# Field attention on one core: four score tiles of a batch issued together, small products and ScalarE's copies placed anew

## What is computed

```python
qkv = (x @ Wqkv.T + bqkv).reshape(Bb, Ss, 3, H, HD).transpose(2, 0, 3, 1, 4)
q, k, v = (qkv[0], qkv[1], qkv[2])
attn = softmax(einsum('bhid,bhjd->bhij', q, k) / sqrt(HD), axis=-1)
coh = sigmoid(tanh(comb @ Wc1.T + bc1) @ Wc2.T + bc2).transpose(0, 2, 1)
mod = attn * coh[..., None]
mod = mod / (mod.sum(-1, keepdims=True) + 1e-08)
mod = (1.0 - fi) * mod + fi * fa[:, None, :, None]
out = einsum('bhij,bhjd->bhid', mod, v).transpose(0, 2, 1, 3).reshape(Bb, Ss, Ee)
return out @ Wout.T + bout
```

## Time and profile before

| | us |
|---|---|
| runs of the kernel | 1911.90, 1923.15, 5402.26 (median 1923.15) |
| span of the profiled execution | 1905.3 |
| field attention in it, first to last exponential | 743.4 to 996 |
| PE busy | 1622.1 (85%) |
| VectorE busy | 1252.2 (66%) |
| ScalarE busy | 1082.6 (57%) |
| GpSimd busy | 861.1 (45%) |

### The profile page before, as it was taken

The page is one execution under the profiler, slowest core; times in us unless marked ns, Lnnn a source line. Parts: engine busy times, 40 slices in busy tenths (PEclk is TensorE's granted clock), DMA queues, the critical chain, the costliest instruction groups (busy, mean ns, idle before and its releaser), DMA issues. The chain is left out here.

```text
span 1905.3 us, 42986 instructions
## 1 busy us (share of the span) xinstructions
PE 1622.1 (85%) x15415; PEld 1160.9 (61%) x15415; DVE 1252.2 (66%) x3295; ACT 1082.6 (57%) x3196; POOL 861.1 (45%) x1080
## 2 busy tenths in 40 slices
PE   3788629983369966999998799999999999899988
PEld 0354329982259953656567677777777777566633
DVE  7588634534454546778876877777777777467757
ACT  2444304431134423889874677777777777777653
POOL 0237746664546641434333866707162543542223
PEclk8799659995579986999989999999999999999989
DMA  2940123314122243000003422231213131221001
GB/s 69 378 150 27 37 62 114 115 56 122 36 63 73 71 129 120 24 28 24 20 21 87 102 62 65 57 73 50 74 40 77 43 87 50 71 54 43 20 13 44
DMA packets 157665, 135.73 MB, mean 71 GB/s; under 512 B 90021, under 2 KB 130278, under 8 KB 155302
## 3 DMA queue, kind: packets, MB, share of 16 engines
q1 hardware_dynamic: 146950, 113.91, 20.3%
q0 software_dynamic: 9088, 18.70, 3.0%
q10 hardware_dynamic: 1440, 0.66, 0.1%
HBM read 76.65 MB, written 56.54 MB: 70 GB/s over the span
## 5 line engine op out<-in xcount | busy, mean ns | idle before, releaser
L847 POOL DMA_INDIRECT y<-moe_y,moe_aim x156 | 177.0, 1135 | 144.5 <-DVE moe_y L987 62.8
L2874 DVE TENSOR_TENSOR delta_sv<-delta_sv,delta_zp 32x256 f32<-32x256 f32 x384 | 161.3, 420 | 111.2 <-PE delta_zp L2440 103.9
L1809 ACT ACTIVATE field_p<-field_sp,field_nm 128x128 f32<-128x128 f32 x512 | 179.9, 406 | 6.7 <-DVE field_nm L1900 6.3
L2787 POOL TENSOR_TENSOR delta_dd<-delta_dd,delta_prod 128x30 f32<-128x30 f32 (+11 forms) x270 | 165.6, 613 | 21.2
L2785 POOL TENSOR_TENSOR delta_prod<-delta_ll,delta_dd 128x30 f32<-128x30 f32 (+11 forms) x270 | 140.5, 520 | 21.2
L2780 POOL TENSOR_TENSOR delta_dd<-delta_ll,delta_minus 128x1024 f32<-128x1024 f32 (+1 forms) x9 | 22.4, 2486 | 270.6 <-DMA delta_ll<-lanes 270.5
L1809 ACT ACTIVATION_READ_ACCUMULATOR field_p<-field_sp,field_nm 128x1 f32 x512 | 126.6, 247 | 0.0
L2440 PE MATMUL delta_zp<-delta_sv,delta_ct 128*32 128x128 f32 x1536 | 121.1, 279 | 5.2 <-DVE delta_sv L2874 4.6
L2858 DVE SCALAR_TENSOR_TENSOR delta_la<-delta_xp,delta_ck,delta_dc 128x256 f32<-128x256 f32 x256 | 107.5, 476 | 3.2 <-PE delta_xp L2398 1.5
L1910 DVE COPY field_pT<-field_ptp 128x512 f32<-128x512 f32 x128 | 84.1, 672 | 33.2 <-PE field_ptp L1659 33.2
L2440 PEld LDWEIGHTS delta_zp<-delta_sv,delta_ct 128*32 128x32 f32 x1536 | 69.6, 109 | 56.2 <-issue 24.3
(11 more groups left out here) (574 smaller groups left out, 4452.3 us busy)
## 6 DMA issues: line engine op xcount, KB each, us to landing
delta_al<-alpha SPq DMA_DIRECT2D x33, 512.0 KB, 4.5
pairs<-c_none SPq DMA_DIRECT2D x16, 1032.0 KB, 17.1
moe_xg<-pairs SPq DMA_DIRECT2D x78, 129.0 KB
moe_yt<-y SPq DMA_DIRECT2D x16, 512.0 KB, 4.7
w_E<-in_E_dram SPq DMA_DIRECT2D x1, 4624.0 KB, 36.1
w_E<-in_E_dram SPq DMA_DIRECT2D x8, 578.0 KB
lanes<-delta_la SPq DMA_DIRECT2D x256, 16.0 KB, 1.5
delta_di<-inverses SPq DMA_DIRECT2D x64, 64.0 KB, 2.3
```

What stands on the lines that cost most here:

```text
L847: nc.gpsimd.indirect_dma_start(results, bass.IndirectOffsetOnAxis(ap=aim[:, t % AR, j:j + 1], axis=0), y[:, t % YS, j, :], None).then_inc( ...
L1809: last = nc.scalar.activation(p[:, slot, h, :], s_ps[i][:, k, :], ACT.Exp, bias=nm[:, slot, h:h + 1], accum_out=zs[:, slot, h:h + 1])
L2787: last = nc.gpsimd.tensor_tensor(dd[lanes, a + 1:, 0:a], dd[lanes, a + 1:, 0:a], pr, ALU.subtract)
L2874: nc.vector.tensor_tensor(sv[rows, two, :], sv[rows, two, :], z_ps[2 * pair // HH][rows, at, :], ALU.subtract).then_inc(s["z_kept"], 1)
```

## The change

PE: `scores` loses its pairs. One call issues all four tiles, and waits until all four tiles of exponentials of the batch before are done. It stands behind `turn(n, 2)` and ahead of `turn(n, 3)`. `turn_factors` goes from the end of batch 0 to its start, `project_t` from its start behind `turn(n, 1)`; the first half of coherence stays at the start of batch 1 (behind the values there); the values of batch 1 and 2 come early in their batch; both halves of `alpha_beta` move up, to either side of `turn(n, 1)` in batch 3; the values of tile 2 come ahead of the scores. ScalarE: `keep_f` moves from batch 1 to batch 0, `keep_k` one tile earlier. VectorE: all four maxima of the next batch come behind the first three copies, `norm_before` comes at the end of a batch, `keep_y` moves from batch 1 to batch 0, `keep_v` ahead of the first copy of batch 3, `norm` ahead of its last two maxima. GpSimd and SyncE are unchanged. Nothing is computed otherwise.

```diff
--- before.py
+++ after.py
@@ -1641,13 +1641,13 @@
             pe.wait_ge(s["xsum_kept"], u + 1)
             nc.tensor.matmul(xa[:, VSUM:VSUM + GB], w["WvT1"][:], xsum[:], start=True, stop=True).then_inc(s["z_made"], 1)
 
-        def scores(n, half, b, pair, group):
-            if b == 0 and pair == 0:
+        def scores(n, half, b, group):
+            if b == 0:
                 pe.wait_ge(s["q_kept"], group + 1)
-            if b < 2 and pair == 0:
+            if b < 2:
                 pe.wait_ge(s["km_made"], group * 2 + 1 + b)
-            pe.wait_ge(s["exps"], n * HQ + 2 * pair + 2 + EXPS0 - HQ)
-            for i in (2 * pair, 2 * pair + 1):
+            pe.wait_ge(s["exps"], n * HQ + EXPS0)
+            for i in range(HQ):
                 rows = slice(i * 32, (i + 1) * 32)
                 nc.tensor.matmul(s_ps[i][:], qT[rows, half, b * T:(b + 1) * T], km[rows, half, :, b * T:(b + 1) * T],
                                  start=True, stop=True).then_inc(s["s_made"], 1)
@@ -1704,8 +1704,7 @@
         project_k(0, 0)
         pe.wait_ge(s["k_kept"], 1)
         project_v(0)
-        scores(0, 0, 0, 0, 0)
-        scores(0, 0, 0, 1, 0)
+        scores(0, 0, 0, 0)
         pe.wait_ge(s["primed"], 1)
         def turn_groups(it):
             for half in range(2):
@@ -1713,56 +1712,55 @@
                 final = isinstance(it, int) and half == 1
                 for b in range(GB):
                     n = u * GB + b
-                    after = (n + 1, half, b + 1) if b < GB - 1 else (n + 1, 1 - half, 0)
                     turn(n, b % 2, 0)
-                    if not final or b < GB - 1:
-                        scores(*after, 0, u if b < GB - 1 else u + 1)
                     if b == 0:
                         pe.wait_ge(s["v_kept"], u + 1)
                         pe.wait_ge(s["h_kept"], u + H0)
+                        turn_factors(u, 1 - half)
+                        values_before(n, 1, 1 - half, GB - 1)
+                    if b == 1:
+                        pe.wait_ge(s["t_kept"], u + 1)
+                        coherence(range(GB // 2))
+                        pe.wait_ge(s["y_kept"], u + 1)
+                        pe.wait_ge(s["vm_made"], (u + 1) * GB)
+                        values_before(n, 0, half, 0)
+                    if b == 2:
+                        values_before(n, 1, half, 1)
+                    if b == 3:
+                        if not final:
+                            pe.wait_ge(s["v_kept"], u + 2)
+                        alpha_beta(u, range(GB // 2))
+                    turn(n, b % 2, 1)
+                    if b == 0:
+                        pe.wait_ge(s["f_kept"], u + 1)
                         project_t(half)
                     if b == 1:
-                        pe.wait_ge(s["t_kept"], u + 1)
-                        pe.wait_ge(s["f_kept"], u + 1)
-                        coherence(range(GB // 2))
-                    if b % 2 == 0:
-                        values_before(n, (b + 1) % 2, half if b else 1 - half, (b - 1) % GB)
+                        coherence(range(GB // 2, GB))
+                        sum_values(u)
                     if b == 2:
                         pe.wait_ge(s["z_kept"], u + 1)
                         if not final:
                             pe.wait_ge(s["k_kept"], u + 2)
                         output(u)
-                    turn(n, b % 2, 1)
-                    if b == 1:
-                        coherence(range(GB // 2, GB))
-                        sum_values(u)
-                        pe.wait_ge(s["y_kept"], u + 1)
-                        pe.wait_ge(s["vm_made"], (u + 1) * GB)
-                        values_before(n, 0, half, 0)
-                        if not final:
-                            project_q(u + 1, 1 - half, it * 16 + 16 + 16 * half, u + 1)
-                    if b == 3 and not final:
-                        pe.wait_ge(s["v_kept"], u + 2)
-                    if b == 3:
-                        alpha_beta(u, range(GB // 2))
-                    turn(n, b % 2, 2)
                     if b == 3:
                         alpha_beta(u, range(GB // 2, GB))
-                    if not final or b < GB - 1:
-                        scores(*after, 1, u if b < GB - 1 else u + 1)
+                    turn(n, b % 2, 2)
+                    if b == 1 and not final:
+                        project_q(u + 1, 1 - half, it * 16 + 16 + 16 * half, u + 1)
+                    if b == 3:
+                        values_before(n, 0, half, 2)
+                    if b < GB - 1:
+                        scores(n + 1, half, b + 1, u)
+                    elif not final:
+                        scores(n + 1, 1 - half, 0, u + 1)
                     turn(n, b % 2, 3)
-                    if b == 0:
-                        pe.wait_ge(s["t_kept"], u + 1)
-                        turn_factors(u, 1 - half)
                     if b == 1 and not final:
                         project_k(u + 1, 1 - half)
                     if b == 2 and not final:
                         pe.wait_ge(s["a_kept"], u + 1)
                         project_v(1 - half)
-                    if b == 3:
-                        values_before(n, 0, half, 2)
-                        if not final:
-                            spread_group(u)
+                    if b == 3 and not final:
+                        spread_group(u)
 
         def spread_group(u):
             pe.wait_ge(s["ba_kept"], u + 1)
@@ -1843,17 +1841,17 @@
                     n = u * GB + b
                     for i in range(HQ):
                         exp_scores(n, b % 2, i)
+                        if b == 0 and i == 1:
+                            keep_f(u)
                         if b == 0 and i == 3:
                             keep_t(u)
-                        if b == 1 and i == 1:
-                            keep_f(u)
                         if b == 1 and i == 3:
                             exp_z(u)
                             if not final:
                                 keep_q(u + 1, 1 - half)
                         if b == 2 and i == 0 and final:
                             alpha_exp(0)
-                        if b == 2 and i == 1 and not final:
+                        if b == 2 and i == 0 and not final:
                             keep_k(u + 1)
                         if b == 2 and i == 3:
                             keep_a(u)
@@ -1967,6 +1965,7 @@
         dve.sem_inc(s["pt_kept"], TURNED0)
         dve.sem_inc(s["h_kept"], H0)
         keep_v(0)
+        norm_before(0, 1)
         for i in range(HQ):
             peaks(0, 0, i)
         before = ch.n
@@ -1978,29 +1977,31 @@
                 for b in range(GB):
                     n = u * GB + b
                     now, then = b % 2, (b + 1) % 2
-                    norm_before(n, then)
                     if b == 2:
                         coherence(u, half)
-                    keep_turned(n, now, 0)
                     if b == 3 and not final:
                         dve.wait_ge(s["vm_made"], (u + 1) * GB)
                         keep_v(u + 1)
+                    keep_turned(n, now, 0)
+                    keep_turned(n, now, 1)
+                    if b == 0:
+                        keep_y(u)
+                        sum_x(u, half, it * 16 + 16)
+                    if b == 1:
+                        keep_z(u)
+                    if b == 3:
+                        keep_alpha(u)
+                    keep_turned(n, now, 2)
+                    norm_before(n + 1, now)
                     if not final or b < GB - 1:
                         for i in range(2):
                             peaks(n + 1, then, i)
-                    if b == 0:
-                        sum_x(u, half, it * 16 + 16)
-                    if b == 1:
-                        keep_y(u)
-                        keep_z(u)
-                    keep_turned(n, now, 1)
-                    keep_turned(n, now, 2)
-                    if b == 3:
-                        keep_alpha(u)
+                    keep_turned(n, now, 3)
+                    if b == 3 and not final:
+                        norm(u)
                     if not final or b < GB - 1:
                         for i in range(2, HQ):
                             peaks(n + 1, then, i)
-                    keep_turned(n, now, 3)
                     if isinstance(it, int) and half == 0:
                         diagonal(ch, range(2 * b, 2 * b + 2))
                     if final and b == 0:
@@ -2010,7 +2011,6 @@
                     if b == 3 and not final:
                         keep_c1(u + 1)
                         scale_alpha(u)
-                        norm(u)
 
         with dve.Fori(0, TURNS - 1) as it:
             ch.turn(it, 2 * LINKS, before)
@@ -2018,7 +2018,6 @@
         assert ch.n == 2 * LINKS, ch.n
         ch.turn(0, 0, before + (GROUPS - 2) * LINKS)
         turn_groups(TURNS - 1)
-        norm_before(B, 1)
         alpha_sum(0)
```

## The result

The changed kernel takes 1942.27 us (median of four runs, 1937.52 to 1946.52). The kernel before took 1911.90, 1914.14 and 1923.15 us, beside the one of 5402.26 that is no measure. Their ratio is 1.0152, with a 95% interval of 1.0123 to 1.0181: slower by 1.5%, some 29 us, and the interval leaves out 1. The forecast was 1948 us.

A forecast was written before the change was run, and what follows sets the result against it. PE's queue was taken to set the 30.58 us beat before. 8 groups x (2.2 + 2.6) = 38 us, less 8, gives +30 on 1917.5: 1948 us, range 1922 to 1973.

The forecast's parts named there:

- PE's saving: In the field stage, joining four score tiles removes 4.2 us a group from PE's queue; none need reach the end.
- The closed ring: Score tiles wait for all four exponential tiles of the batch before: 7.56 us a batch, 31.29 a group with two copies.
- PE late: PE's queue makes scores late by 0.55 us in batch 1 and 0.93 in batch 3; batches 0 and 2 on time.
- Other queues: Norm in batch 3 stays hidden: input ready about 9.2 us after the batch's first exponential, VectorE arrives at 9.5.
- Sum without drops: Field stage beat from handovers, copies and PE's lateness at full clock: 32.8 us a group, +2.2.
- Drops: PE's clock falls in nearly every batch 3, four of five batches 1, 3.4 us each: 2.6 us a group lost.
- What before pays: In the field stage the kernel before loses about 8 us to its own clock drops, subtracted from the added time.
- What would show it: ScalarE waits 1 to 2 us a batch, beat 32.8 to 36 us, PE busy below 85%, clock falling in most groups.
- the ring without drops: Rival: field stage without clock drops, 8 x 2.2 - 8 = +10 us, 1928 us; chance 0.22.
- Long drops: Rival: half or all of batch 3's clock drops last 10 us, 1962 to 1975 us; chance 0.20.
- The gain: Rival: handover costs much less, beat about 27.5 us a group, -25 us, 1893 us; chance 0.05.
- the tiles do run side by side: Rival denied this: the second score pair lands 1.06 us later, +33 us, 1950 us; chance 0.05.

The follow-up runs named there:

- e3_ahead: Changed kernel with four unread transposes a batch between the wait for the exponentials and the scores; 1.0323 of the kernel before.
- e4_behind: Changed kernel with four unread transposes a batch ahead of the first transposes, where PE waits; 1.0127 of the kernel before.
- e1_pairs: Changed kernel with scores in two pairs, the first waiting only for exponential tiles 0 and 1, and two maxima ahead of norm_before; 1.0085 of the kernel before.
- e9_values: Changed kernel with batch 3's values of tile 2 right behind the first transposes instead of ahead of the scores; 1.0102 of the kernel before.
- e2_filled: Changed kernel with unread transposes of the identity where PE would wait; 1.0051 of the kernel before.
- e5_alone: Kernel before with four score tiles together where pair 1 stood, and VectorE's first two maxima and fourth copy reordered to follow; 1.0266 of the kernel before.
- e6_one: Kernel before with four score tiles together in batch 1 only, its values moved behind project_k; 0.9993 of the kernel before.
- e7_two: e6_one with four score tiles together also in batch 0; 1.0116 of the kernel before.
- e10_best: e6_one with values first in batch 2, f copied one tile earlier and all coherence products in one piece; 1.0017 of the kernel before.
- e11_repairs: Kernel before, score pairs everywhere, with values first in batch 2, f copied one tile earlier and coherence products in one piece; 1.0149 of the kernel before.

## Why the prediction was right

The forecast was +1.6% and +30 us; it came to +1.5% and, within the stage, +29.6 us. The ring is right in its mechanism and its size. The clock's term is right in its total alone, and there by luck. Step by step:

- **PE's saving.** 4.2 us a group were to vanish from PE's queue, worth nothing. The x8 row takes 1.08 us; PE's busy time fell by 10.7 us over the kernel, less than 8 x 4.2. Half clock explains at most 10 of the missing 23 us (by the traces' records of the clock the stage had 41.0 us at the lower level, before 20.5); the rest is open. None of the saving reached the end. The Trainium skill (TensorEngine Tiling (Array Packing), section PSUM Bottleneck) has the emptying of PSUM as what can bound tiled matmuls. The trace agrees in part: TensorE's gain is lost at the banks, but to a ring of handovers, 2.49 us in a batch, and not to the emptying engine's load (ScalarE is busy 22.81 of 30 us).
- **The closed ring.** Forecast 7.56 us a batch. The one batch with no copy inside and no lateness, batch 1 of the last group, took 7.64. The handover measured 0.60 + 1.16 + 0.73 = 2.49 against 2.43. k adds 0.57 (8.21) as forecast, f 0.49 (8.13) against 0.48. e3_ahead and e4_behind show the ring directly, and e1_pairs opens it. The batch of 7.64 us is a single one, so its closeness to the forecast is weak evidence by itself.
- **PE late.** Batch 1: 8.22 - 7.64 = 0.58 against 0.55. Batch 3 without a drop: 8.66 - 7.64 = 1.02 against 0.93.
- **Other queues.** The norm stretches the way from the first to the second maxima row from 1.81 us (845.54 to 847.35) to 2.40 (857.25 to 859.65), and ScalarE is busy 4.00 of 4.00 us at 858 to 862: hidden, as forecast.
- **Sum without drops.** 8.13 + 8.22 + 8.21 + 8.66 = 33.22 us a group, forecast 32.8: 0.4 too little, 3 us over 8 groups.
- **Drops.** Forecast 2.6 us a group: 1.5 in batch 3 and 1.1 in batch 1. The seven distances from tanh to tanh sum to 251.7 us; less 7 x 33.22 that is 19.2 us, or 2.7 a group. The total was right, its two terms were not. Batch 3 lost 10.2 - 8.66 = 1.6 us in a short drop and 11.7 - 8.66 = 3.0 in a long one, over the seven 16 us, 2.3 a group. Batch 1 lost 11.21 - 8.22 = 3.0 us in the first group and nothing in the others, 0.4 a group: the term "four of five batches 1" is the step that failed, and with it the term of 3.4 us for every drop, since three of seven in batch 3 lasted 6.8. PE's wait of 1.79 us was there as forecast (867.74), and the small products behind it, but the clock held. The reason that I had at hand, values of 1.08 us behind the first small products, doesn't stand, since in e9_values the same order dropped. The prediction's rule, a wait and then small products, thus names a place where drops come often but doesn't say when. Its reading of before at 980 us was loose as well: that drop began at 980.54 by the clock's record, inside the wait of 1.14 us that it is said to follow. Two errors of opposite sign cancelled; that the total is right is luck.
- **What before pays.** 32.75, five of 30.6 and 36.62 sum to 222.3 us; less 7 x 30.58 that is 8.2, forecast 8. But the forecast was 6.0 for the one long beat and 1.7 for the drop at 980, which lies behind the last tanh; the 8.2 are 6.0 and the 2.2 of the first beat. It is also a figure of one execution: in 18 runs of before, spans go from 1904.4 us at a mean clock of 0.910 to 1923.6 at 0.898, so its own drops differ from run to run.
- **What would show it.** One wait of ScalarE a batch of 1.09 and 1.36 us (forecast 1 to 2), PE busy 82% of 800 to 830 us (below 85%), beats of 34.8 to 36.3 us but for the first of 39.58 (32.8 to 36). The clock fell in every group but the last, in batch 3 and, only in the first group, in batch 1, where both were forecast for most groups.
- **The whole.** Over the seven distances: 7 x (33.22 - 30.58) = 18.5 for ring and lateness, 16 + 3 = 19 for the drops, taken from the batches, less 8.2: 29.3. Measured: 251.7 - 222.3 = 29.4. This shows how the loss divides and proves nothing more, since its terms come from the same trace. The forecast's +30 stood for eight groups; the last one has less to wait for.

The rivals: the ring without drops (1928 us) is nearly what e2_filled is, with one drop left, at 1.0051, 10 us above before, as its +10 says. Long drops came in three of seven batches 3, of 6.8 us where 10 was forecast, and didn't reach 1962. The gain didn't come through, and the tiles do run side by side. More went wrong in my expectations of variants. For e3_ahead and e5_alone, drops in batch 1 were missing. For e6_one, PE's new waits were. For e7_two it was PE's lateness in batch 0, the wait for f and drops in batch 1. For e10_best and e11_repairs it was the wait that the earlier copy of f makes, and in e11_repairs drops again. The clock was misjudged most often, but waits that an edit opens were too.

## What to carry to other kernels

Joining matmuls that run side by side frees the engine that issues them, but it also makes the first of them wait for what only the last one needs. With one set of banks that closes a ring: add up the handovers (here 2.5 us a batch) before adding up the saving (here 1.06). Look at the waits that it opens in TensorE's queue and at what stands behind them: drops of the clock there cost as much (19 us over seven groups) as ring and lateness did (18.5). The same holds for a repair: an instruction moved ahead must find its input ready, or it holds up what now stands behind it (1.5 us in e10_best and e11_repairs).

## What the hardware showed unexpectedly

More work on TensorE made the kernel faster: 360 unread transposes took it from 1.0152 to 1.0051, and the drops from eight to one. An edit in batch 3 moved the clock's drops to batch 1 (e9_values). And drops came in two lengths, 3.4 and 6.8 us, after what looks like the same queue: seven batches 3 took 11.87, 10.22, 11.70, 10.24, 10.21, 11.75 and 10.64 us in one execution. Why one is long stays open. The Trainium skill (TensorE: Matmul & The Clock Gate, section A second HAM failure mode) tells of short idles between groups of matmuls that make the clock swing; e2_filled agrees: with these idles filled the clock was 1.00 in both stretches shown, and one drop was left in the stage.
